# A two-layer graph kernel whose pair order, step schedule, weight expansion and bias load are rearranged

## The reference, cut to what matters

```python
def _ggc(x, adj, W, wih, whh, bih, bhh):
    m = adj @ (x @ W)
    gi = m @ wih.T + bih
    gh = x @ whh.T + bhh
    i_r, i_z, i_n = jnp.split(gi, 3, axis=-1)
    h_r, h_z, h_n = jnp.split(gh, 3, axis=-1)
    r = jax.nn.sigmoid(i_r + h_r)
    z = jax.nn.sigmoid(i_z + h_z)
    n = jnp.tanh(i_n + r * h_n)
    return (1.0 - z) * n + z * x
h = jax.nn.relu(_ggc(x, adj, W1, ...))
x = _layernorm(x + jax.nn.relu(_ggc(h, adj, W2, ...)))
# last layer
support = x @ weight
mask = (adj != 0)
rank = jnp.cumsum(mask, axis=1)
deg = rank[:, -1:]
k = jnp.minimum(deg, 100.0)
pos = rank - (deg - k)
w = mask * jnp.where(pos > 0, 0.5 ** (k - pos), 0.0)
x = _layernorm(x + w @ support + bias)
```

## Time and profile before

| what | value |
|---|---|
| median of 3 runs | 444.81 us (441.56 to 445.54) |
| the profiled execution's own time | 445.22 us |
| its span | 443.4 us |
| TensorE busy | 370.8 us, 84% |
| VectorE busy | 300.4 us, 68% |
| ScalarE busy | 154.9 us, 35% |
| GpSimd busy | 25.6 us, 6% |
| transfers | 120.53 MB, mean 272 GB/s |
| mean granted TensorE clock | 0.94 |

### The profile page before, as it was taken

The page is one execution under the profiler, slowest core; times in us unless marked ns, Lnnn a source line. Parts: engine busy times, 40 slices in busy tenths (PEclk is TensorE's granted clock), DMA queues, the critical chain, the costliest instruction groups (busy, mean ns, idle before and its releaser), DMA issues.

```text
span 443.4 us, 6443 instructions
## 1 busy us (share of the span) xinstructions
PE 370.8 (84%) x2424; PEld 177.0 (40%) x2424; DVE 300.4 (68%) x466; ACT 154.9 (35%) x186; POOL 25.6 (6%) x32
## 2 busy tenths in 40 slices
PE   5499889898989998998888876949969898597864
PEld 2142232333324342432332433425434445576854
DVE  2378889687686684774726284362967979856793
ACT  0004112121302121211210626226284775785793
POOL 1000000000000000000001010100101010101042
PEclk9889999999999999999999695988989999988996
DMA  7699999999999898979999480784959993000011
GB/s 261 246 387 388 376 398 380 405 342 394 328 381 330 327 383 271 405 251 350 378 370 402 149 329 0 257 337 141 366 217 352 383 365 111 13 1 1 2 49 49
DMA packets 37614, 120.53 MB, mean 272 GB/s; under 512 B 4816, under 2 KB 9040, under 8 KB 37584
## 3 DMA queue, kind: packets, MB, share of 16 engines
q1 hardware_dynamic: 37584, 120.12, 73.9%
HBM read 118.00 MB, written 1.05 MB: 268 GB/s over the span
## 4 chain that ended last, share of the span: by engine, by line
PE 47%; DMA 22%; DVE 15%; ACT 7%; issue 6%; SPq 1%; POOL 0%; POOLq 0%; DVEq 0%; ACTq 0%
PE m_acc L377 22%; DMA stream<-in_adj_t 22%; PE out L377 9%; DVE run L831 6%; PE out L476 4%; DVE codes L836 4%; PE rz_ps L449 3%; ACT codes L645 3%; ACT wexp L645 2%; PE rz_ps L434 2%; PE n_ps L434 2%; PE rz_ps L476 2%; PE n_ps L476 1%; DVE codes L795 1%; DVE x1s L939 1%
## 5 line engine op out<-in xcount | busy, mean ns | idle before, releaser
L377 PE MATMUL m_acc<-stream,s_in 128*64 128x512 f32 x512 | 131.0, 617 | 19.6 <-DMA stream<-in_adj_t 18.9
L795 DVE TENSOR_SCALAR codes<-stream 128x1024 uint8<-128x1024 f32 x128 | 84.2, 687 | 27.4 <-DMA stream<-in_adj_t 26.8
L377 PE MATMUL m_acc<-stream,s_mid 128*64 128x512 f32 x304 | 74.5, 626 | 4.5 <-DMA stream<-in_adj_t 4.5
L377 PEld LDWEIGHTS m_acc<-stream,s_in 128*64 128x64 f32 x512 | 34.8, 139 | 88.0 <-issue 45.2
L645 ACT ACTIVATE wexp<-codes,code_bias 128x2048 uint16<-128x2048 uint8 x24 | 47.3, 1992 | 32.6 <-DVE codes L836 32.5
L377 PE MATMUL out<-stream,s_mid 128*64 128x512 f32 x208 | 54.1, 596 | 4.2 <-DMA stream<-in_adj_t 4.2
L736 POOL TENSOR_TENSOR rstd<-var,mhalf 128x4 f32<-128x4 f32 x16 | 23.7, 1484 | 414.1 <-DVE var L932 414.1
L377 PEld LDWEIGHTS m_acc<-stream,s_mid 128*64 128x64 f32 x304 | 20.7, 143 | 48.6 <-issue 46.6
L836 DVE SCALAR_TENSOR_TENSOR codes<-codes,run 128x1024 uint32<-128x1024 uint32 x32 | 39.2, 1225 | 1.2
L831 DVE TENSOR_TENSOR run<-run,codes 128x2048 uint16<-128x2048 uint16 x31 | 37.9, 1224 | 1.6
L864 DVE SCALAR_TENSOR_TENSOR t_n<-n_ps,const,rz 128x256 f32<-128x256 f32 x16 | 7.7, 483 | 41.0 <-ACT rz L599 41.0
(11 more groups left out here) (137 smaller groups left out, 353.8 us busy)
## 6 DMA issues: line engine op xcount, KB each, us to landing
stream<-in_adj_t SPq DMA_DIRECT2D x218, 512.0 KB, 7.2
hx<-in_x_pairs SPq DMA_DIRECT2D x8, 128.0 KB, 7.8
mx<-in_x_t SPq DMA_DIRECT2D x8, 128.0 KB, 6.8
mx<-hx SPq DMA_DIRECT2D x16, 64.0 KB, 5.8
x_res<-in_x_pairs SPq DMA_DIRECT2D x8, 128.0 KB, 5.4
out_nodes<-stream SPq DMA_DIRECT2D x8, 128.0 KB, 1.9
const<-in_consts SPq DMA_DIRECT2D x1, 358.0 KB, 8.1
bias_b<-in_bias SPq DMA_DIRECT2D x1, 128.0 KB, 13.0
```

The costliest lines, as they stand in the source:

```text
L377: last = nc.tensor.matmul(to[D * u:D * (u + 1), :], state[:, t * D:(t + 1) * D], stream[:, n % SLOTS, u * CW:(u + 1) * CW], start=start[u] ...
L795: nc.vector.tensor_scalar(edges(q // 2, b, 2 * (q % 2), 2), stream[:, n % SLOTS, :], 0.0, None, ALU.not_equal).then_inc(mask_made, 1)
```

## The change

Pairs used twice rise from 2 * 19 to 2 * 22 (`TRI`), and the loads fall from 218 to 212. In pass 1 the pairs of chunks 2 to 7 are taken in a written order, twice-used ones between others; `QUADS` and `NEED` make the mask sums follow that order. The first four chain tiles are begun in pass 1 for the first six target chunks (`CHAIN_EARLY`), and done for the last two chunks behind it. The turn has 11 pairs, and each step t = 1 to 6 has gates, then 12 pairs (13 in the last), with the node's matmuls and the four shares at fixed places early in the step. The chain is one source chunk further ahead, the ring for the first 20 blocks has three places (half of `s_in` or `kept` is the third), and ScalarE expands the next step's first blocks. The 44 last shares, `BY_ACT` and `BY_DVE` (47 and 17) have another order, and the state and the residual's input are issued separately. The bias comes from the host as 128 rows of 1 KB.

```diff
-TRI = (0, 0, 1, 2, 3, 4, 4, 5)
+TRI = (0, 0, 2, 3, 4, 4, 4, 5)
...
+BY_TURNS = [0, 8, 1, 9, 2, 10, 3, 11, 4, 12, 5, 13, 6, 14, 7, 15]
+PAIRS = [list(range(NP)), list(range(NP)),
+         [0, 4, 1, 5, 8, 9, 10, 11, 6, 12, 7, 13, 2, 14, 3, 15],
+         [0, 8, 1, 9, 2, 10, 3, 11, 6, 12, 7, 13, 4, 14, 5, 15],
+         BY_TURNS, BY_TURNS, BY_TURNS,
+         [0, 10, 1, 11, 2, 12, 3, 13, 4, 14, 5, 6, 7, 15, 8, 9]]
+QUADS = [(slice(0, 2), slice(2, 4), slice(4, 6), slice(6, 8))] * 2 + \
+    [(slice(0, 4, 2), slice(4, 6), slice(1, 4, 2), slice(6, 8))] + \
+    [(slice(0, 2), slice(4, 6), slice(2, 4), slice(6, 8))] * 4 + \
+    [(slice(0, 2), slice(5, 7), slice(2, 4), slice(4, 8, 3))]
+NEED = [(8, 12, 16)] * 2 + [(8, 15, 16)] * 5 + [(8, 13, 16)]
 TURN = [(0, 10), (0, 11), (0, 12), (0, 13), (1, 8), (1, 9), (1, 10), (1, 11), (1, 12),
-        (0, 14), (0, 15), (1, 13), (1, 14), (1, 15)]
-LOADS = [(b, q) for b in range(NCH) for q in range(NP)] + [(NCH + s, q) for s, q in TURN] + \
+        (0, 14), (0, 15)]
+LOADS = [(b, q) for b in range(NCH) for q in PAIRS[b]] + [(NCH + s, q) for s, q in TURN] + [(NCH + 1, q) for q in (13, 14, 15)] + \
         [(NCH + s, q) for s in range(2, NCH) for q in range(2 * TRI[NCH - 1 - s], NP)]
 LOAD_AT = {pair: n for n, pair in enumerate(LOADS)}
 USED = [1 + max(n for n, (g, q) in enumerate(LOADS) if g == step) for step in range(2 * NCH)]
...
+FOLD, TO_BF, COUNT, START = 1, 3, 5, 6
...
+EARLY = NCH - 2
+CHAIN_EARLY = {6: {12: 1, 14: 1}, 7: {9: 1, 12: 1}}
+N_EARLY = sum(sum(n.values()) for n in CHAIN_EARLY.values())
+ALONG_PAIRS = {1: 12, 2: 12, 3: 12, 4: 12, 5: 12, 6: 13}
+FIRST = [NCH * NP, *(NCH * NP + len(TURN) + sum(ALONG_PAIRS[u] for u in range(1, t))
+                     for t in range(1, NCH))]
+STATE_AT = [FIRST[1] - 1, *(n + SLOTS for n in FIRST[1:NCH - 1]), len(LOADS)]
+RES_AT = [FIRST[1], *(n + SLOTS + 3 for n in FIRST[1:NCH - 1]), len(LOADS)]
...
 ORDER = [(t - 2, i) for t in range(2, 7) for i in range(ALONG)] + \
-    [(5, 0), (5, 1), (0, 4), (1, 4), (2, 4), (3, 4), (4, 4), (5, 2), (5, 3), (5, 4),
-     (0, 5), (1, 5), (2, 5), (3, 5), (4, 5), (5, 5), (6, 0), (6, 1), (6, 2), (6, 3),
-     (6, 4), (6, 5)] + [(j, 6) for j in range(7)] + [(7, i) for i in range(7)] + \
-    [(j, 7) for j in range(NCH)]
+    [(0, 4), (1, 4), (2, 4), (3, 4), (4, 4), (5, 0), (5, 1), (5, 2), (5, 3),
+     (0, 5), (1, 5), (2, 5), (3, 5), (6, 0), (6, 1), (6, 2), (6, 3), (5, 4), (6, 4), (4, 5),
+     (7, 0), (7, 1), (7, 2), (7, 3), (7, 4), (5, 5), (6, 5), (7, 5)] + \
+    [(j, 6) for j in range(NCH)] + [(j, 7) for j in range(NCH)]
+GATES_END, NODES_END = [(0, 4), (0, 5)], [(3, 4), (3, 5)]
 AT = {block: n for n, block in enumerate(ORDER)}
 RING = 5 * ALONG
-AHEAD = [(0, 4), (1, 4), (2, 4), (3, 4), (4, 4), (0, 5), (1, 5), (2, 5), (3, 5)]
+NODE_AT = {1: 5, 2: 3, 3: 3, 4: 3, 5: 3, 6: 3}
+SHARE_AT = {2: (0, 1, 4, 6), 3: (0, 1, 4, 6), 4: (0, 1, 4, 6), 5: (0, 1, 4, 6), 6: (0, 1, 4, 6)}
+AHEAD = [(0, 4), (1, 4), (0, 5), (2, 4), (1, 5), (3, 4), (2, 5), (4, 4), (3, 5)]
...
-PLACE = {block: f"w{n % 2}" for n, block in enumerate(ORDER[:RING])}
-PLACE.update({block: f"d{1 + n}" for n, block in enumerate(AHEAD)})
+PLACE = {block: ("w0", "w1", "x" if n < 3 * ALONG else "k")[n % 3]
+         for n, block in enumerate(ORDER[:RING])}
+PLACE.update({block: f"d{n}" for n, block in zip((1, 3, 2, 5, 4, 7, 6, 9, 8), AHEAD)})
 PLACE.update({block: (PLACES + AGAIN + AGAIN)[n] for n, block in enumerate(REST)})
-BY_DVE = [REST[n] for n in (6, 8, 10, 12, 14, 15, 17, 18, 20, 22, 24, 26, 28, 30, 32, 34)]
-BY_ACT = [(0, 0), (0, 1), (0, 2), (0, 3), (1, 0), (1, 1), (1, 2), (1, 3), (2, 0), (2, 1),
-          AHEAD[0], (2, 2), (2, 3), (3, 0), (3, 1), AHEAD[1], AHEAD[2],
-          (3, 2), (3, 3), (4, 0), (4, 1), AHEAD[3], AHEAD[4],
-          (4, 2), (4, 3), REST[0], REST[1], AHEAD[5], AHEAD[6]] + \
-    [block for block in REST[2:8] if block not in BY_DVE] + AHEAD[7:] + \
-    [block for block in REST[8:] if block not in BY_DVE]
-ACT_EXPANDS = {1: (0, 0, 2), 2: (1, 1, 2), 3: (1, 1, 3), 4: (1, 1, 4), 5: (1, 1, 4),
-               6: (1, 1, 4), 7: (1, 1, 5), 8: (1, 1, 4)}
+BY_DVE = [REST[n] for n in (4, 6, 8, 10, 12, 14, 15, 17, 18, 20, 22, 24, 26, 28, 30, 32, 34)]
+BY_ACT = [(0, 0), (0, 1), (0, 2), (0, 3), (1, 0), (1, 1), (1, 2), AHEAD[0]] + \
+    [block for j in range(1, 4) for block in
+     [(j, 3), (j + 1, 0), (j + 1, 1), AHEAD[2 * j - 1], (j + 1, 2), AHEAD[2 * j]]] + \
+    [(4, 3), REST[0], REST[1], AHEAD[7], AHEAD[8]] + \
+    [block for block in REST[2:] if block not in BY_DVE]
+ACT_EXPANDS = {1: (0, 0, 3), 2: (1, 1, 3), 3: (1, 1, 4), 4: (1, 1, 4), 5: (1, 1, 4),
+               6: (1, 1, 3), 7: (1, 1, 2), 8: (1, 1, 3)}
 DVE_EXPANDS = {1: (0, 0, 0), 2: (0, 0, 0), 3: (0, 0, 0), 4: (0, 0, 0), 5: (0, 0, 0), 6: (0, 0, 0),
-               7: (0, 0, 1), 8: (2, 1, 5)}
-ACT_END = (1, 1, 1, 1, 0, 1, 1, 0)
+               7: (0, 0, 3), 8: (2, 1, 4)}
+ACT_END = (1, 1, 1, 1, 1, 1, 1, 0)
...
+PLACE_USED = {f"s{i}": 1 + max(n for n in range(len(LOADS)) if n % SLOTS == i)
+              for i in range(SLOTS)}
+PLACE_USED.update({"m": len(LOADS), "x": NCH * NP, "k": USED[2 * NCH - 4] + 1})
...
+def codes_count(j, k, late=True):
+    n = KT * j + KT - 1 - k
+    return n + 1 + (N_EARLY if late else 0)
+CHAIN = [chain_tiles(*x) for x in ((0, 4), (4, 8), (8, 12), (12, 16), (16, 20), (20, 25), (25, 30),
+                                   (30, 32), (32, 32))]
...
+            if place == "x":
+                return s_in[:, NT * D // 2:].bitcast(BF16)
+            if place == "k":
+                return kept[:, :, :].rearrange("p a i -> p (a i)").bitcast(BF16)
...
+            def load_res(s):
+                ch, g = NCH - 1 - s, NCH + s
                 if s > 0:
                     sp.wait_ge(h_made, g)
                 sp.dma_start(x_res[:, :], x_pairs[:, bass.ts(ch, HW)]).then_inc(x_c_in, 16)
                         load_x(q // 2 + 1)
                     if b == 0 and q == 4:
                         sp.dma_start(const[:, :], consts).then_inc(consts_loaded, 16)
-                        sp.dma_start(bias_b[:, :, :], bias).then_inc(consts_loaded, 16)
+                        sp.dma_start(bias_b[:, :, :].rearrange("p k d -> p (k d)"), bias).then_inc(consts_loaded, 16)
             for n in range(NCH * NP, len(LOADS)):
-                if n == NCH * NP + len(TURN) - 1:
-                    state2(0)
-                for s in range(2, NCH):
-                    if n == USED[NCH + s] - 1:
-                        state2(s - 1)
                 load(n)
+                for s in range(NCH):
+                    if n == STATE_AT[s]:
+                        state2(s)
+                    if n == RES_AT[s]:
+                        load_res(s)
             state2(NCH - 1)
+            load_res(NCH - 1)
             for i in range(NCH):
                 if i in OUT_ACT:
...
-                last = pair(n, q, s_in, m_acc[b % 2], [q == 0] * 2, q == NP - 1)
-                if q < 2 * TRI[b]:
+                last = pair(n, q, s_in, m_acc[b % 2], [q == PAIRS[b][0]] * 2, q == PAIRS[b][-1])
+                twice = [p for p in PAIRS[b] if p < 2 * TRI[b]]
+                if q in twice:
+                    first = q == twice[0]
                     pe.wait_ge(s_mid_made, q // 2 + 1)
-                    if q == 0:
+                    if first:
                         if b == 3:
                             pe.wait_ge(to_sup_made, 4)
                         if b - 2 in KEPT:
                             pe.wait_ge(m2_kept, KEPT.index(b - 2) + 1)
-                    end = q == 2 * TRI[b] - 1
-                    last = pair(n, q, s_mid, m2_bank(b), [q == 0] * 2, end and b in KEPT)
+                    last = pair(n, q, s_mid, m2_bank(b), [first] * 2, q == twice[-1] and b in KEPT)
                 last.then_inc(pair_used, 1)
...
             for n, (s, q) in enumerate(TURN):
                 product2(s, q)
+                if n == 1:
+                    gates(NCH - 1)
                 if n == 2:
-                    gates(NCH - 1)
-                if n == 3:
                     count(NCH - 1)
-                if n == 6:
+                if n == 5:
                     node(NCH - 1)
-            gates(NCH)
-            for n, q in enumerate(range(2 * TRI[NCH - 3], NP)):
-                if n == 7:
-                    node(NCH)
-                product2(2, q)
-            def chunk2(t):
-                s, j = t + 1, t - 2
-                pairs = [(s, q) for q in range(2 * TRI[NCH - 1 - s], NP)]
-                ahead = 2 if t == 2 else 0
-                for pair_at in pairs[:ahead]:
-                    product2(*pair_at)
+            def chunk2(t, first):
                 gates(NCH + t - 1)
-                share(j, 0)
-                share(j, 1)
-                for pair_at in pairs[ahead:6]:
-                    product2(*pair_at)
-                node(NCH + t - 1)
-                share(j, 2)
-                mid = (len(pairs) + 6) // 2
```

(81 more changed lines are left out.)

55 lines of the change are left out of this document (26 added, 29 removed).

## The result

| | before | changed |
|---|---|---|
| median | 444.44 us (4 runs) | 377.89 us (377.27 to 378.18, 4 runs) |
| ratio | | 0.8509, 95% interval 0.8467 to 0.8552 |
| span of the profiled execution | 443.4 us | 376.4 us |
| TensorE busy | 370.8 us, 84% | 350.5 us, 93% |
| VectorE busy | 300.4 us | 301.3 us |

The account below looks back on a forecast made before the run. One late transfer bounds the start, transfers or TensorE pass 1, transfers the turn; pass 2 waits for expansions and codes. Span 231.7 + 91 + 62 = 384.7 us, execution 1.8 longer: 387 us, range 377 to 408.

Parts of the forecast that it names:

- Bias: At the start, the late bias load: 4 us gained, bounds 0 and 6.00 us.
- Pass 1: Pairs by turns, six more used twice: last four stretches from 100.2 to 97 us, 3 gained; bounds 6 gained, 4 lost.
- Rival 3: Pass 1 gets longer, VectorE's backlog freeing slots late, 7 us lost: 397; chance 0.18 shared with one other rival.
- Turn: From chunk 7's gates to step 1's: 31.1 us taken as 30.5; step 0's uncovered gates cost nothing, 2 if slots are full.
- Steps: Steps 2 to 6 of pass 2: 18.2 us a step, 91 for five, against 130.4.
- each loses something to the others: Steps 2 to 6: TensorE, transfers, VectorE and ScalarE nearly equal, so 18.2 us a step where TensorE needs 17.6.
- Rival 1: Steps run at 22.4 us, weights, codes and slots still meeting late: 408; chance 0.13.
- The codes are made in the step in which they are used.: Pass 2: expansions wait 8.06 us for VectorE's codes, and TensorE stands 7.38 us before the first shares.
- End: Behind step 6's gates: 13, then 18, then 24 us, with 6.2 more 61 to 62, against 72.3.
- Rival 2: The end keeps its 72 us, paced by expansions whatever their order: 397; chance 0.18 shared with one other rival.
- Rival 4: TensorE at 1.2 GHz through pass 2, short groups in different banks: slower, 387 + 135; chance 0.04.
- Rival 5: Codes come in the old step after all, only bias and loads count: about 435; chance 0.05.

Follow-up runs that it names:

- the two bias runs: Changed kernel with the old bias load: 383.28 us (0.8624); old kernel with only the new bias load: 438.16 us (0.9854).
- The direct experiment: Changed kernel with twice-used pairs in a row, single ones behind, in chunks 4 to 7 of pass 1: 383.15 us (0.8615).
- The experiment on the expansions' lead: Changed kernel with ScalarE expanding a source chunk's four blocks in the step that uses them, codes still a step ahead: 420.42 us (0.9459).
- the attempt with the later node: Changed kernel with the last node's matmuls behind share (6, 1) in place of before (3, 5): 376.85 us (0.8498).
- the order experiment: Changed kernel with the old order of the 44 last shares and old places of the last two gates and nodes: 394.53 us (0.8872).

## Why the prediction was right, point by point

The forecast was 387 us, measured 377.9, inside the range and only 0.9 us from its low end. The signs named for it came: no wait of TensorE over 3 us between 20 and 320 us, steps of 17.8 to 19.1 us at clock 1.00, no wait of ScalarE for codes, a transfer share of 1.04 in 12 to 20 us, and 11.3 us between the last two gates. In terms of the span the forecast was 384.7 and 376.4 came: 5.3 us better up to the gates of chunk 7 and 5.1 better at the end, 0.8 worse in the turn and 1.4 in the steps. So the mechanism of the largest piece, the steps, and its size were right; both ends were underestimated, and that the misses stayed inside the range is in part luck.

- *Bias.* 4 forecast, 5.4 measured. Rows 1 gave 4.1 us of lost engine time in 12 to 20 us against a full share of 1; without the late load the share there is 1.04, which makes it 4.4 to 4.6. The last 0.8 us isn't located. By the rule in the Trainium skill, "DMA: Bandwidth & Descriptors", section "Rules for kernel authors", a transfer whose outer dimension is a multiple of 16, as 128 is here, isn't confined to few engines, and I took that to mean no gain. The trace doesn't contradict the rule, as up to 12 packets were under way at once; what failed is my step from it to a time, which the two bias runs refute, and my reading of rows 1 as few engines. The forecast of 4 us did not need that reading.
- *Pass 1.* Gates of chunk 7 forecast at 201.2, came at 195.9. Of these 5.3 us, 1.2 lie before the gates of chunk 1, 1.6 in chunks 2 and 3, for which I had no gain, and 2.5 in the last four stretches: they went from 100.4 to 93.5, where 3 and 1.4 less were forecast. The mis-sized term there is the loss I left on top of TensorE's work: four chunks of 23.8 us are 95.2, and I took 97; nothing was lost. The 0.88 us a pair was slightly high as well: it takes 0.86, and the chunk 23.6. The direct experiment gives 5.3 for the order alone, where I had 3. The gain of chunks 2 and 3 was not tested by itself. Rival 3, loads held up by VectorE, is ruled out: without the early tiles pass 1 was as long.
- *Turn.* 30.5 forecast, 31.3 measured. The term put at nothing is the uncovered gates of step 0: TensorE waited 1.46 us there, and the turn came out 0.8 us over the forecast.
- *Steps.* 91 forecast, 92.4 measured, at clock 1.00, ScalarE not waiting for codes. But the bound is TensorE alone; "each loses something to the others" was wrong: nothing was lost, where I had 3 us for it in five steps, and TensorE's own work was 0.2 to 1.5 us a step more than my 17.6, 4.4 in five. Shares and pairs beside each other cost 1.00 and 1.01 us (0.94 and 0.88 in my rows), some 0.6 a step; to start the bank I had 0.5, and it is a matmul group of 1.00 us in steps 2 and 3 and none in the others; the last step has a 13th pair, 0.86. The two errors nearly cancelled, which is luck. Of the 39 us I gave 7 to fewer pairs and the rest to the wait and its clock. The experiment on the expansions' lead shows that with the wait back nothing is left of the gain, though the pairs are still fewer; the 7 were not tested by themselves. Rival 1 is ruled out.
- *"The codes are made in the step in which they are used."* That is too simple. In the old kernel they are finished behind the gates of the step that uses them, at the end of VectorE's list of the step before, and ScalarE starts then. Of the two leads, the expansions' is the one that counts.
- *End.* 62 forecast, 56.9 measured. Gates of step 7 came 11.3 us behind those of step 6 (13 forecast, 20.4 before), the first finished chunk 18.6 later (18), the last stretch 20.8 (24). The mis-sized term is the last, which I had paced by expansions. When the first chunk is finished there are more shares left than before: 347 matmul records fall in the last stretch, 223 in the old one, and TensorE is busy 19.7 of 20.2 us (15.5 of 20.7 before). So it is the shares that fill it, with the expansions close behind: where the wait in front of them shrank (the attempt with the later node), new waits came. Rival 2, that the order doesn't matter, is ruled out by the order experiment.
- *Rival 4.* The clock is 1.00 in steps whose groups alternate about every microsecond; the oscillation that the Trainium skill, "TensorE: Matmul & The Clock Gate", section "A second HAM failure mode: psum-queue depth-cycling", tells of did not come. *Rival 5* needs nothing more.

What the parts cost when taken back one at a time adds up to 5.4 + 5.3 + 5.1 + 42.5 + 2.2 + 16.6 = 77.1 us, against a gain of 66.6: they overlap. Not tried alone are the six loads fewer, the third place in the ring, the early places of node and shares in a step, and the separate issue of state and residual input.

## What to carry to other kernels

A wait of TensorE costs more than its length: waits of 5.7 us made a step 8.3 us longer, since the work behind them ran at 1.2 GHz. So look for the room to prepare an operand one whole step ahead of its use (here a third place in the ring) before shaving the operations themselves. Where an engine's busy time equals the stretch, see what stands right behind it before cutting its work: here an order that saved TensorE 0.3 to 0.7 us a step only moved the wait to the loads. A small transfer in an odd layout early in a transfer-bound stage can delay everything behind it: here one that landed some 5 us later cost 5.4 to 6.5 us at the end.

## What the runs showed of the hardware that was not expected

- 128 KB read as 512 repeats of a 256-byte row took 13.0 us to land and left the transfer share at 0.47 to 0.48 for 8 us; as 128 rows of 1 KB it took 8.1 us at a share of 1.04. The 256-byte packets were short, 15 ns each, and far apart.
- A group of 16 float16 matmuls and one of 4 float32 matmuls take 1.00 and 1.01 us when they alternate; in runs of their kind they take 0.89 and 0.86.
- Transfers run at a share near 1.0 at anything between 329 and 403 GB/s, so the rate alone doesn't say whether they are the bound.
